# Attention stage: one normalisation and a fifth factor head move from VectorE to GpSimd, and some steps change their head

## Chip, cores and metric

One core of a Trainium2 chip runs the whole kernel. The metric is the device time of one execution in microseconds; lower is better. Engines are called by their names in the profile: PE is TensorE (PEld its weight loads), DVE VectorE, ACT ScalarE, POOL GpSimd, SP the queue that issues DMAs.

## What is computed

Four residual stages over x of 8 x 1024 rows of 256; the change touches only the first, attention with a learned relation bias:

```python
q, k, v = (x @ W.T + b).reshape(b, s, h, hd)          # 16 heads of 16
attn_scores = einsum('bihd,bjhd->bhij', q, k) / scale
logits = li[:, :, None, :] + lj[:, None, :, :] + rel_b # 3 relations per pair (i, j)
relation_probs = softmax(logits)
bias = einsum('bijk,hk->bhij', relation_probs, logical_bias)
gate = sigmoid(x @ gate_W.T + gate_b)
attn_weights = softmax(attn_scores + gate * bias)
out = einsum('bhij,bjhd->bihd', attn_weights, v) @ Wo.T + bo
x = x + out                                            # attention's x is layernorm(x)
```

An fp8-like linear layer, a Mamba mixer and a tail of MLPs follow; they are the same before and after.

## The kernel before, in words

Attention works in 64 tiles t of 128 query rows against the 1024 keys of their batch. Every engine runs its own hand-written list of steps per tile, `body`, in which `u` counts the 16 heads; semaphores alone tie the lists together. Two tiles are one turn of a loop.

For head h the steps are: the factor pass f(h), which writes rho[h] * P1 + P0 into one of eight row buffers `srow`. VectorE does it in one instruction from PSUM (`dve_f`, L491). For the heads in POOL_HEADS, 1, 4, 8 and 12, GpSimd does it in two from SBUF (`pool_f`, L408 and L410), with a wait on its own first result between them and a wait for the row buffer's last transposes (t_ok). Then s(h), `dve_s` (L502): add the scores from PSUM `ps_s`, of which there is only one, and take the row's minimum. VectorE's order is f(u+1), s(u), extras of u, so between s(u) and s(u+1) lie the extras of u and f(u+2). PE's next scores (L647) wait for s(u). Then e(h) on ScalarE (L576), the exponential with that minimum; eight transposes on PE (L658), which come two heads behind; their copies by ScalarE (L585); and PE's product with V (L670).

Beside this each tile t prepares two other tiles. The relation factors of tile t+1: `dve_rel` at u = 0 and 1 (L474, L477) write RT; GpSimd `pool_rel` (L382, twice), ScalarE `act_rel` at u = 1, 3, 4; GpSimd `pool_sum` (L387, L391); ScalarE `act_y0` at u = 7 and 8, Ln and Exp (L568, L571), of which R2 is an approximate reciprocal; then a Newton pass: GpSimd `pool_t` (L395), VectorE `dve_y` at u = 10 (L482); then GpSimd's two products `pool_p` (L400), which raise p_ok. ScalarE's `act_p` (L537, u = 13) copies one of them into PSUM `ps_p`, for VectorE's f(0) of the next tile.

The projections of tile p = t+9: `dve_ln` at u = 2 (L432, L434, L436: mean, variance), GpSimd `pool_rstd` (L368), VectorE `dve_xn` at u = 5 (L440), PE's transposes and products through the one PSUM bank `ps_m`, ScalarE `act_d` (eT, L528), GpSimd `pool_gT` (L414: eT becomes min(eT, HUGE) + 1), VectorE `dve_qk` at u = 14 (L447, waits for gT_ok and for PE), and in the next tile ScalarE `act_hi` (L542), GpSimd `pool_rem` (L372), `act_mid`, `pool_lo` (L376). `dve_v` (L455, u = 4) adds V's bias, `pool_ge` (L418), `dve_gate` (u = 13) and `pool_kappa` (L422) make the gate. The output of tile t-1: `act_o` (L589, u = 5) copies ps_o, `dve_norm` (L508, L510) divides, `pool_xrb` (L427) adds the bias to the residual, `dve_out` adds the rest. The last eight tiles have no projections (`pro` is false).

GpSimd's order in a tile is: f(4), rem, rel, rel, rstd, lo, f(8), sum, sum, f(12), xrb, t, ge, p, p, eT, f(1) of the next tile, kappa.

Of the kernel before, what the change touches and what calls it, by code (L numbers as in the profile page):

```python
# [18 lines left out]
NT = S // P  # L19
# [30 lines left out]
def attention(nc, x_in, wqk, wvg, bqk, rows, ident_in, parts_d, x_out):  # L50
# [4 lines left out]

    AHEAD = NT + 1
    NROW = 8
    POOL_HEADS = (1, 4, 8, 12)
    DVE_HEADS = tuple(h for h in range(H) if h not in POOL_HEADS)
    NPH, NDH = len(POOL_HEADS), len(DVE_HEADS)  # L60
    LAG = 2
# [2 lines left out]
    with ExitStack() as ctx:  # L64
# [301 lines left out]
        def pool_rstd(pool, p):  # L366
            alone(pool, ln_step, 3 * p + 3, pool_own)
            nc.gpsimd.tensor_tensor(rstd[:], ve[:], mhalf[:], ALU.pow).then_inc(rstd_ok, 1)  # L368

        def pool_rem(pool, p):  # L370
            alone(pool, hi_ok, p + 1, pool_own)
            nc.gpsimd.tensor_tensor(qkf[:], qkf[:], parts[:, 0], ALU.subtract).then_inc(rem_ok, 1)  # L372
# [57 lines left out]
        def dve_ln(dve, p, k):  # L430
            wait(dve, x_in_s, 16 * p + 16)
            nc.vector.bn_stats(stats[:], xt[:, k, :]).then_inc(ln_step, 1)  # L432
            alone(dve, ln_step, 3 * p + 1, dve_own)
            nc.vector.bn_aggr(mv[:], stats[:]).then_inc(ln_step, 1)  # L434
            dve.wait_ge(ln_step, 3 * p + 2)
            nc.vector.tensor_scalar(ve[:], mv[:, 1:2], LN_EPS, None, ALU.add).then_inc(ln_step, 1)  # L436

        def dve_xn(dve, p, k):
            wait(dve, rstd_ok, p + 1)
            nc.vector.tensor_scalar(xn[:], xt[:, k, :], mv[:, 0:1], rstd[:, 0:1],  # L440
                                    ALU.subtract, ALU.mult).then_inc(x_free, 1)

        def dve_qk(dve, p):
            wait(dve, gT_ok, p + 1)
# [404 lines left out]
        @block.gpsimd  # L849
        def _(pool):  # L850
            def start(pool):
                pool_g_rstd(pool, 0)
                pool_rstd(pool, NT)
                pool_g_rstd(pool, 1)
                pool_gT(pool, NT)
                pool_rem(pool, NT)
                pool_lo(pool, NT)
                pool_f(pool, 0, 0, 1)

            def body(pool, t, k, par, ib, pro, post, look, before):  # L860
                pool_f(pool, t, k, 4)
                if followed(t, pro):
                    pool_rem(pool, t - 1 + AHEAD)
                for n in range(2 * look):
                    pool_rel(pool, t + 1, 1 - k, after(par, ib, 1), n)
                if pro:
                    pool_rstd(pool, t + AHEAD)
                if followed(t, pro):
                    pool_lo(pool, t - 1 + AHEAD)
                pool_f(pool, t, k, 8)  # L870
                for n in range(2 * look):
                    pool_sum(pool, t + 1, 1 - k, n)
                pool_f(pool, t, k, 12)
                if post:
                    pool_xrb(pool, t - 1)
                if look:
                    pool_t(pool, t + 1)
                if pro:
                    pool_ge(pool, t + NT)
                for n in range(2 * look):  # L880
                    pool_p(pool, t + 1, 1 - k, n)
                if pro:
                    pool_gT(pool, t + AHEAD)
                if look:
                    pool_f(pool, t + 1, 1 - k, 1)
                if pro:
                    pool_kappa(pool, t + NT, 1 - par, ib)

            def finish(pool):
                pool_xrb(pool, TILES - 1)  # L890

            nc.gpsimd.memset(mhalf[:], -0.5)
            for v in V:
                nc.gpsimd.memset(v[:, :, :, HD + 1:2 * HD], 0.0)
                nc.gpsimd.memset(v[:, :, :, HD:HD + 1], 1.0).then_inc(v_ok, 1)
            pool.wait_ge(v_ok, 2)
            run(pool, start, body, finish)

        @block.vector
        def _(dve):  # L900
# [51 lines left out]
            def body(dve, t, k, par, ib, pro, post, look, before):  # L952
                for u in range(H):
                    if u + 1 < H:
                        dve_f(dve, t, k, u + 1)
                    dve_s(dve, t, k, after(par, ib, 0), u)
                    if look and u < 2:
                        dve_rel(dve, t + 1, 1 - k, after(par, ib, 1), u)
                    if pro and u == 2:
                        dve_ln(dve, t + AHEAD, 1 - k)  # L960
                    if u == 3 and (not isinstance(t, int) or t >= 2):
                        dve_out(dve, t - 2)
                    if pro and u == 5:
                        dve_xn(dve, t + AHEAD, 1 - k)
                    if pro and u == 4:
                        dve_v(dve, t + NT, 1 - par, ib)
                    if post and u == 6:
                        dve_norm(dve, t - 1)
                    if look and u == 10:
                        dve_y(dve, t + 1)  # L970
                    if pro and u == 13:
                        dve_gate(dve, t + NT)
                    if pro and u == 14:
                        dve_qk(dve, t + AHEAD)
                    if look and u == 15:
                        dve_f(dve, t + 1, 1 - k, 0)
# [48 lines left out]
            for i, (c, sgn, inv) in enumerate(((cdiff[:, 0, :], csgn, cn), (cdT[:], sgT, cdT))):  # L1025
# [10 lines left out]
                                    w_qk[:, :, 0:D].rearrange("p c (h d) -> p c h d", d=HD),  # L1036
                                    cinv[:].unsqueeze(1).unsqueeze(3).broadcast_to([P, DC, H, HD]), ALU.mult
                                    ).then_inc(w_ready, 1)
            dve_xn(dve, NT, 0)
            dve_g_ln(dve, 1)  # L1040
            dve_g_xn(dve, 1)
            dve.wait_ge(w_ready, 2)
# [2 lines left out]
        @block.scalar  # L1045
        def _(act):
            def start(act):
                act.wait_ge(w_ready, 1)
                act_g_t(act, 0)
                act_xT(act, NT)  # L1050
                act_g_d(act, 0)
                act_g_e(act, 0)
                act_d(act, NT, NT)
                for s in range(2):
                    act_g_hi(act, 0, s)
                act_g_t(act, 1)
                for s in range(2):
                    act_g_mid(act, 0, s)
                act_g_ge(act, 0)
                act_g_d(act, 1)  # L1060
                act_g_e(act, 1)
                act_rel(act, 0, 0, 0, 0)
                act_rel(act, 0, 0, 0, 1)
                act_rel(act, 0, 0, 0, 2)
                for s in range(2):
                    act_g_hi(act, 1, s)
                for s in range(2):
                    act_g_mid(act, 1, s)
                for step in range(2):
                    act_y0(act, 0, step)  # L1070
                act_p(act, 0, 0)
                act_hi(act, NT)
                act_g_ge(act, 1)
                act_mid(act, NT)
                act.wait_ge(g_st, 16 * 8)

            def body(act, t, k, par, ib, pro, post, look, before):
                for u in range(H):
                    act_e(act, t, u)
                    if post and u == 5:  # L1080
                        act_o(act, t - 1)
                    if pro and u == 7:
                        act_xT(act, t + AHEAD)
                    if look and u in (7, 8):
                        act_y0(act, t + 1, u - 7)
                    if u >= LAG:
                        act_at(act, t, u - LAG)
                    elif post:
                        act_at(act, t - 1, H + u - LAG)
                    if u == 0 and (not isinstance(t, int) or t >= 2):  # L1090
                        act_aT(act, t - 2)
                    if followed(t, pro) and u == 0:
                        act_hi(act, t - 1 + AHEAD)
                    if followed(t, pro) and u == 2:
                        act_mid(act, t - 1 + AHEAD)
                    if look and u in (1, 3, 4):
                        act_rel(act, t + 1, 1 - k, after(par, ib, 1), (1, 3, 4).index(u))
                    if pro and u == 6:
                        act_gate(act, t + NT, 1 - par, ib)
                    if pro and u == 10:  # L1100
                        act_d(act, t + AHEAD, after(par, ib, AHEAD))
                    if look and u == 13:
                        act_p(act, t + 1, 1 - k)

            def finish(act):
                for u in range(H - LAG, H):
                    act_at(act, TILES - 1, u)
                act_aT(act, TILES - 2)
                act_o(act, TILES - 1)
                act_aT(act, TILES - 1)  # L1110

            act.preload_act_table_set("natural_log_exp_and_others")
            act.sem_inc(at_ok, 2)
            run(act, start, body, finish)
# [1298 lines left out]
```

## Time and profile before

| | us |
|---|---|
| median of 3 runs (lowest, highest) | 6042.34 (6040.91, 6044.29) |
| the profiled execution | 6042.3 |
| its span, first to last instruction | 6040.5 |
| busy in the span: PE, DVE, ACT, POOL | 5365.8, 4701.5, 4409.7, 3704.9 |

Attention takes about the first 2850 us of the span. The granted clock of PE is 1.00 through its middle. A timeline row gives start, duration, engine, line, operation, output <- inputs with partitions x elements, a count, and in brackets the idle time just before it and what ended it. Successive instructions of one engine overlap a little, so steps are best read from start to start.

### The profile page before, as it was taken

The numbers are of one execution on the slowest core, as the hardware profiler recorded it, in microseconds if no ns is written. First come the engines' busy times: TensorE is split into PE (matmuls) and PEld (weight loads), VectorE is DVE, ScalarE is ACT, GpSimd is POOL, SyncE is SP. The second block draws the span as 40 slices with busy tenths as digits, with TensorE's granted clock in tenths as the row PEclk, the third lists the DMA queues.
The fourth block names the chain that finished last, engine by engine and source line by source line (L and its number), as shares of the span: only waits on it lengthen the run. The fifth ranks groups of instructions, "written<-read, shape, count | busy, mean of one in ns | idle before, by whom it ended". The sixth has DMA issues, their size and how long they took to land. (4 is left out here: it accounts for less than half of the span.)

```text
span 6040.5 us, 114022 instructions
## 1 busy us (share of the span) xinstructions
PE 5365.8 (89%) x40162; PEld 3532.6 (58%) x40162; DVE 4701.5 (78%) x6099; ACT 4409.7 (73%) x7005; POOL 3704.9 (61%) x2010
## 2 busy tenths in 40 slices
PE   6888888898989898888799869999999979999999
PEld 4666666666666666655344345555555546666665
DVE  6999999999999999998888679999999942122221
ACT  4999999999999999999366678888888821111111
POOL 3888888888888888875100079999999930000000
PEclk8999999999999999999899889999999989999999
DMA  2121121212112121200355555555555521111110
GB/s 74 28 49 31 28 51 28 51 28 51 28 34 45 30 48 31 46 17 14 129 190 211 187 211 187 208 208 191 195 201 207 184 101 42 45 35 35 35 35 11
DMA packets 461255, 537.80 MB, mean 89 GB/s; under 512 B 237537, under 2 KB 337761, under 8 KB 460785
## 3 DMA queue, kind: packets, MB, share of 16 engines
q1 hardware_dynamic: 460784, 531.75, 28.0%
q8 instruction: 268, 4.39, 0.3%
q14 instruction: 203, 1.66, 0.1%
HBM read 370.31 MB, written 161.35 MB: 88 GB/s over the span
## 5 line engine op out<-in xcount | busy, mean ns | idle before, releaser
L502 DVE CUSTOM_DVE_ANT_0 srow<-srow,ps_s,small 128x1024 f32<-128x1024 f32 x1024 | 1304.0, 1273 | 63.5 <-issue 34.6
L576 ACT ACTIVATE srow<-srow,nmax 128x1024 f32<-128x1024 f32 x1024 | 1200.0, 1172 | 87.3 <-DVE nmax L502 78.3
L585 ACT COPY AT<-ps_t 128x512 f32<-128x512 f32 x2048 | 1110.5, 604 | 19.8 <-PE ps_t L658 18.8
L658 PEld LDWEIGHTS ps_t<-ident,srow 128*128 128x128 f32 x8192 | 954.9, 141 | 224.2 <-issue 36.3
L658 PE MATMUL ps_t<-ident,srow 128*128 128x128 f32 x8192 | 1068.7, 273 | 2.8 <-ACT AT L585 2.4
L1977 POOL TENSOR_TENSOR c_hc<-c_hs,c_cs 128x1024 f32<-128x1024 f32 x432 | 1009.9, 2364 | 61.2 <-DVE c_hs L2079 59.1
L491 DVE SCALAR_TENSOR_TENSOR srow<-ps_p,rho,R 128x1024 f32<-128x1024 f32 x768 | 975.3, 1270 | 0.0
L1938 PE MATMUL c_ps_y<-c_hc,c_ident 128*128 128x512 f32 x2048 | 944.8, 594 | 29.9 <-DVE c_y L2062 21.4
L2079 DVE TENSOR_TENSOR_SCAN c_hs<-c_da,c_pd 128x1024 f32<-128x1024 f32 x384 | 860.1, 2273 | 54.6 <-PE c_pd L1929 54.6
L647 PE MATMUL ps_s<-K,Q 96*128 96x512 bf16 x2048 | 617.1, 383 | 291.2 <-DVE nmax L502 265.3
L2022 ACT ACTIVATE c_sT<-c_dxT,c_bT 128x256 f32<-128x256 f32 x1536 | 668.4, 494 | 107.0 <-PE c_pd L1929 96.9
L410 POOL TENSOR_TENSOR srow<-srow,R 128x1024 f32<-128x1024 f32 x256 | 608.1, 2375 | 46.9 <-POOL srow L408 46.9
L670 PE MATMUL ps_o<-AT,V 128*32 128x128 f32 x16384 | 607.4, 278 | 0.0
L2215 POOL TENSOR_TENSOR d_rstd<-d_ve,d_mhalf 128x4 f32<-128x4 f32 x16 | 16.3, 1017 | 899.1 <-DVE d_ve L1222 899.1
L1938 PEld LDWEIGHTS c_ps_y<-c_hc,c_ident 128*128 128x128 f32 x2048 | 359.5, 190 | 344.9 <-issue 314.0
L1929 PEld LDWEIGHTS c_pd<-c_ident,c_sT 128*128 128x128 f32 x3072 | 353.9, 142 | 340.0 <-issue 198.1
L1929 PE MATMUL c_pd<-c_ident,c_sT 128*128 128x128 f32 x3072 | 407.4, 276 | 106.8 <-DVE c_hc L2086 79.6
L670 PEld LDWEIGHTS ps_o<-AT,V 128*32 128x32 f32 x16384 | 401.3, 109 | 129.3 <-issue 128.5
L2013 ACT ACTIVATE c_da<-c_dt,c_a_neg 128x1024 f32<-128x1024 f32 x384 | 435.8, 1135 | 1.7 <-issue 1.7
L647 PEld LDWEIGHTS ps_s<-K,Q 96*128 96x128 bf16 x2048 | 144.4, 97 | 476.0 <-DVE nmax L502 342.9
L1970 POOL TENSOR_TENSOR c_db<-c_dx,c_bs 128x1024 f32<-128x1024 f32 x128 | 302.1, 2361 | 121.4 <-DMA c_bs<-bc_d 121.4
L2242 DVE TENSOR_TENSOR d_x<-d_ps_y,d_y 128x512 f32<-128x512 f32 x32 | 22.1, 691 | 438.6 <-PE d_ps_y L2317 438.6
(256 smaller groups left out, 8576.5 us busy)
## 6 DMA issues: line engine op xcount, KB each, us to landing
c_cs<-bc_d SPq DMA_DIRECT2D x256, 512.0 KB, 4.3
c_bs<-bc_d SPq DMA_DIRECT2D x64, 512.0 KB, 6.5
Q<-parts_d SPq DMA_DIRECT2D x384, 64.0 KB, 2.3
parts_d<-parts SPq DMA_DIRECT2D x57, 384.0 KB, 3.4
K<-parts_d SPq DMA_DIRECT2D x168, 128.0 KB, 4.4
sz_d<-b_sz SPq DMA_DIRECT2D x16, 1024.0 KB, 7.1
xv_d<-b_xv SPq DMA_DIRECT2D x16, 1024.0 KB, 7.8
dt_d<-b_ab SPq DMA_DIRECT2D x16, 1024.0 KB, 4.2
```

The source lines that it names most:

```text
L491: nc.vector.scalar_tensor_tensor(r[:], ps_p[:], rho[:, h:h + 1], R[k][0][:], ALU.mult, ALU.add).then_inc(fd_ok, 1)
L502: nc.vector.tensor_tensor_reduce(r[:], r[:], ps_s[:], small[:, slot, h:h + 1], BIG, ALU.add, ALU.min, nmax[:, h % NROW:h % NROW + 1]).then ...
L576: nc.scalar.activation(r[:], r[:], ACT.Exp, scale=-1.0, bias=nmax[:, h % NROW:h % NROW + 1]).then_inc(e_ok, 1)
L585: nc.scalar.copy(AT[h % NAT][:, HG * half:HG * half + HG, :], ps_t[:, half]).then_inc(at_ok, 1)
L647: last = nc.tensor.matmul(ps_s[:, n * 512:(n + 1) * 512], Q6[k][:, h, :], K6[:, h, n * 512:(n + 1) * 512], start=True, stop=True)
L658: last = nc.tensor.transpose(ps_t[:, half, i, :], rows_sb[h % NROW][:, j * P:(j + 1) * P], ident[:])
L670: last = nc.tensor.matmul(ps_o[32 * i:32 * i + 32, j, :], V[par][:, n, h, :], AT[h % NAT][:, n, :], start=(n == 0), stop=(n == NT - 1))
L1929: last = nc.tensor.transpose(pd[:, c, k * P:(k + 1) * P], src[:, k, c * P:(c + 1) * P], ident[:])
L1938: last = nc.tensor.matmul(ps_y[:, c, cut], ident[:], hc[place((n, c)) % NHC][:, cut], start=n == 0, stop=n == NS - 1)
L1977: nc.gpsimd.tensor_tensor(hc[place((n, c)) % NHC][:], hs[place((n, c)) % NHS][:], cs[n % NCS][:], ALU.mult).then_inc(hp_ok, 1)
L2022: last = nc.scalar.activation(sT[i % NSC][:, k, :], dxT[p][:, k, :], ACT.Copy, scale=bT[p][:, k, n:n + 1])
L2079: nc.vector.tensor_tensor_scan(h, gain, push, 0.0, ALU.mult, ALU.add).then_inc(h_ok, 1)
```

## The change

GpSimd takes the factor passes of heads 1, 4, 7, 10 and 13 instead of 1, 4, 8 and 12; VectorE does f(8) and f(12) and no longer f(7), f(10) and f(13). The normalised x (`xn`) is written by GpSimd (`pool_xn`), right after rstd and after a wait on its own result. `dve_ln` waits for the xn before (x_free) ahead of overwriting mean and variance. On VectorE V's bias goes from u = 4 to 5, the Newton pass `dve_y` from u = 10 to 11; on ScalarE the copy of ps_o goes from u = 5, just after e(5), to the end of u = 4. GpSimd's order becomes: f(4), rem, rel, rel, rstd, xn, lo, f(7), sum, sum, f(10), t, f(13), ge, xrb, p, p, eT, f(1), kappa.

```diff
-    POOL_HEADS = (1, 4, 8, 12)
+    POOL_HEADS = (1, 4, 7, 10, 13)
+        def pool_xn(pool, p, k):
+            alone(pool, rstd_ok, p + 1, pool_own)
+            nc.gpsimd.tensor_scalar(xn[:], xt[:, k, :], mv[:, 0:1], rstd[:, 0:1],
+                                    ALU.subtract, ALU.mult).then_inc(x_free, 1)
...
         def dve_ln(dve, p, k):
             wait(dve, x_in_s, 16 * p + 16)
             nc.vector.bn_stats(stats[:], xt[:, k, :]).then_inc(ln_step, 1)
+            alone(dve, x_free, p + 2, dve_own)
             alone(dve, ln_step, 3 * p + 1, dve_own)
...
-        def dve_xn(dve, p, k):
-            wait(dve, rstd_ok, p + 1)
-            nc.vector.tensor_scalar(xn[:], xt[:, k, :], mv[:, 0:1], rstd[:, 0:1],
-                                    ALU.subtract, ALU.mult).then_inc(x_free, 1)
...
                 if pro:
                     pool_rstd(pool, t + AHEAD)
+                    pool_xn(pool, t + AHEAD, 1 - k)
                 if followed(t, pro):
                     pool_lo(pool, t - 1 + AHEAD)
-                pool_f(pool, t, k, 8)
+                pool_f(pool, t, k, 7)
                 for n in range(2 * look):
                     pool_sum(pool, t + 1, 1 - k, n)
-                pool_f(pool, t, k, 12)
+                pool_f(pool, t, k, 10)
+                if look:
+                    pool_t(pool, t + 1)
+                pool_f(pool, t, k, 13)
+                if pro:
+                    pool_ge(pool, t + NT)
                 if post:
                     pool_xrb(pool, t - 1)
-                if look:
-                    pool_t(pool, t + 1)
-                if pro:
-                    pool_ge(pool, t + NT)
...
                     if pro and u == 5:
-                        dve_xn(dve, t + AHEAD, 1 - k)
-                    if pro and u == 4:
                         dve_v(dve, t + NT, 1 - par, ib)
                     if post and u == 6:
                         dve_norm(dve, t - 1)
-                    if look and u == 10:
+                    if look and u == 11:
                         dve_y(dve, t + 1)
...
-                    if post and u == 5:
-                        act_o(act, t - 1)
...
+                    if post and u == 4:
+                        act_o(act, t - 1)
```

The prologue's one `dve_xn` becomes a `pool_xn` in GpSimd's `start` in the same way.

## Rows read from the trace of the kernel before

**Rows 1.** Busy us (x instructions) of each engine, 1500 to 2000 us; then clock, DMA
```profile
1500.00:2000.00 500.00, 447.29 (x5386) 337.28 (x5385) 474.41 (x691) 485.64 (x742) 422.50 (x256) 1.00 0.16 35
```

**Rows 2.** Timeline of ScalarE, one tile: start us, us, engine line, [idle before]
```profile
1191.10 1.15 ACT L576 ACTIVATE srow<-srow,nmax 128x1024 f32<-128x1024 f32 x1 [0.46 <-DVE nmax L502]
...
1205.88 1.07 ACT L568 ACTIVATE R<-RT 128x1024 f32<-128x1024 f32 x1
...
1208.84 1.08 ACT L571 ACTIVATE R<-R 128x1024 f32<-128x1024 f32 x1
...
1234.38 1.15 ACT L576 ACTIVATE srow<-srow,nmax 128x1024 f32<-128x1024 f32 x1 [0.46 <-DVE nmax L502]
```

**Rows 3.** Timeline of GpSimd over the same tile
```profile
1202.35 2.38 POOL L391 TENSOR_TENSOR RT<-RT,R 128x1024 f32<-128x1024 f32 x1 [0.27 <-POOL RT L387]
1204.70 1.12 POOL L408 TENSOR_SCALAR srow<-R,rho 128x1024 f32<-128x1024 f32 x1
...
1208.34 0.74 POOL L427 TENSOR_TENSOR xr<-xr,row 128x256 f32<-128x256 f32 x1
1210.09 2.38 POOL L395 TENSOR_TENSOR RT<-RT,R 128x1024 f32<-128x1024 f32 x1 [1.01 <-ACT R L571]
1212.44 0.28 POOL L418 TENSOR_SCALAR ge<-ge 128x16 f32<-128x16 f32 x1
1213.91 4.72 POOL L400 TENSOR_TENSOR R<-R,R 128x1024 f32<-128x1024 f32 x2 [1.19 <-DVE R L482]
1218.61 1.06 POOL L414 TENSOR_SCALAR eT<-eT 128x256 f32<-128x256 f32 x1
...
1223.29 0.23 POOL L422 TENSOR_TENSOR small<-cn,gate 128x16 f32<-128x16 f32 x1
...
1230.74 2.23 POOL L372 TENSOR_TENSOR qkf<-qkf,parts 128x512 f32<-128x512 f32 x1 [2.93 <-ACT parts L542]
```

**Rows 4.** Timeline of VectorE, end of this tile and start of the next
```profile
1222.73 0.61 DVE L447 SCALAR_TENSOR_TENSOR qkf<-ps_m,b_qk,eT 128x128 f32<-128x128 f32 x2 [0.37 <-PE ps_m L613]
...
1223.59 1.27 DVE L502 CUSTOM_DVE_ANT_0 srow<-srow,ps_s,small 128x1024 f32<-128x1024 f32 x1
...
1227.48 0.88 DVE L474 TENSOR_SCALAR RT<-Dj,small 128x1024 f32<-128x1024 f32 x1
...
1230.68 1.27 DVE L477 SCALAR_TENSOR_TENSOR RT<-Dj,small,RT 128x1024 f32<-128x1024 f32 x1
...
1233.07 1.26 DVE L502 CUSTOM_DVE_ANT_0 srow<-srow,ps_s,small 128x1024 f32<-128x1024 f32 x1
```

**Rows 5.** Timeline of VectorE: the Newton pass, V's bias and xn
```profile
1212.51 1.23 DVE L482 SCALAR_TENSOR_TENSOR R<-RT,R 128x1024 f32<-128x1024 f32 x1 [0.18 <-POOL RT L395]
...
1239.65 0.42 DVE L455 TENSOR_TENSOR V<-ps_m,row 128x256 f32<-128x256 f32 x1 [0.41 <-PE ps_m L635]
...
1242.47 0.64 DVE L440 TENSOR_SCALAR xn<-xt,mv,rstd 128x256 f32<-128x256 f32 x1
```

**Rows 6.** VectorE against GpSimd: timeline rows, and L372's ns min/median/max
```profile
93.42 2.35 POOL L410 TENSOR_TENSOR srow<-srow,R 128x1024 f32<-128x1024 f32 x1 [0.18 <-POOL srow L408]
...
94.56 2.29 DVE L477 SCALAR_TENSOR_TENSOR RT<-Dj,small,RT 128x1024 f32<-128x1024 f32 x1
...
L372 POOL TENSOR_TENSOR qkf<-qkf,parts x57: 1152/2233/2252, 84.9 to 2529.1; 128x512 f32<-128x512 f32 x57
...
2734.96 2.36 POOL L410 TENSOR_TENSOR srow<-srow,R 128x1024 f32<-128x1024 f32 x1 [0.18 <-POOL srow L408]
...
2736.66 1.22 DVE L474 TENSOR_SCALAR RT<-Dj,small 128x1024 f32<-128x1024 f32 x1
```

**Rows 7.** Timeline of GpSimd in two of the last tiles, which project nothing
```profile
2719.91 2.36 POOL L395 TENSOR_TENSOR RT<-RT,R 128x1024 f32<-128x1024 f32 x1 [1.51 <-ACT R L571]
...
2762.00 2.37 POOL L395 TENSOR_TENSOR RT<-RT,R 128x1024 f32<-128x1024 f32 x1 [1.52 <-ACT R L571]
```

More of the change, by code:

```diff
@@ L853, in start @@
                 pool_rstd(pool, NT)
+                pool_xn(pool, NT, 0)
                 pool_g_rstd(pool, 1)
@@ L1038, in _ @@
                                     ).then_inc(w_ready, 1)
-            dve_xn(dve, NT, 0)
             dve_g_ln(dve, 1)
```

## The prediction

> **What bounds the kernel now.** Only the attention stage is touched, so I first read the busy time of the engines over 500 us in its middle [rows 1]: ScalarE 485.6 of 500, VectorE 474.4, TensorE 447.3, GpSimd 422.5. No engine is free, and ScalarE alone would need 0.971 of the time. The order of events decides, so I read the timeline of one tile, engine by engine. Call s(h) the VectorE reduction of head h (L502), f(h) the factor pass in front of it (L491 on VectorE, L408 with L410 on GpSimd), e(h) ScalarE's exponential (L576). The same e(2) of two tiles starts at 1191.10 and 1234.38 [rows 2]: a period of 43.28 us, and 64 tiles make the stage. The loop that closes this period runs as follows. e(2) waits 0.46 us for VectorE; from there ScalarE never stops until Ln (L568) at 1205.88 and Exp (L571) at 1208.84 [rows 2]. GpSimd's product pool_t waits for that Exp and starts at 1210.09 [rows 3]. Then GpSimd sits idle 1.19 us for VectorE's Newton pass (L482), does the two products of L400 and eT (L414), and reaches f(1) of the next tile [rows 3]. VectorE's qkf (L447) starts at 1222.73, s(15) follows at 1223.59, and s(2) of the next tile at 1233.07 [rows 4], which frees e(2) at 1234.38. GpSimd has one large slack, 2.93 us before L372, where it has run ahead of ScalarE [rows 3].
>
> **The change, part by part, in one tile.** *VectorE loses* one factor pass of the twelve and xn, 0.64 us [rows 5], and dve_v one head later no longer meets its 0.41 us wait for TensorE [rows 5]. A factor pass costs about 1.2 us: from L502 at 1223.59 to L474 at 1227.48 [rows 4] there are three such passes, s(15), f(0) and s(0), with a wait of 0.2 among them, in 3.89. That is 2.2 us less, from 41.1 us busy. But nothing of it counts if VectorE then waits at L447.
>
> *GpSimd gains* a factor pass, 3.64 us (1204.70 to 1208.34 [rows 3]), and xn. The trace shows no subtract-and-multiply on GpSimd with two column scalars. Nearest rows: mult-and-add of 1024 columns 1.12, and of 16 columns (min, add) 0.28; interpolated, 256 columns are 0.28 + 0.84/4 = 0.5. Against it min-and-add of just 256 columns takes 1.06 [rows 3]. Bounds 0.28 and 1.06; I take 0.5, since arithmetic without a min is nearer to L408, plus 0.18 for the wait on its own previous result, as L410 shows in front of it [rows 6]. Is it on the path? The sums (L391) end at 1202.35 + 2.38 = 1204.73, and Ln starts at 1205.88, held by ScalarE's own work: 1.15 of cover. 0.18 + 0.5 + 0.05 for a semaphore fits. Above 0.9 us xn would come through; at 1.06 it costs 0.17 per tile. The Trainium skill (GPSIMD Engine Reference, § 4.1 Engine selection) calls one-input work on GpSimd roughly line rate; L408 agrees, L414 with a quarter of the columns in the same 1.1 us does not. By the rule the sum below stands at 6112; by L414 it would be 6122.
>
> *The new order on GpSimd.* Between Exp and eT stood pool_t, ge, an idle wait for the Newton pass, two products, eT. Now it is pool_t, f(13), ge, xrb, two products, eT. The idle wait goes (the Newton pass finds f(13) as cover), but 3.64 + 0.74 comes in. Chain from e(2):
> - to Ln 14.78, to the start of pool_t 4.21 (1210.09 - 1205.88) [rows 2, 3]: unchanged, ScalarE's own pace
> - pool_t 2.35, f(13) 3.64, ge 0.28, xrb 0.74, products 4.70 (1213.91 to 1218.61), eT 1.06 [rows 3]: 12.77
>
> So eT is ready 31.76 after e(2). Today L447 starts 1222.73 - 1191.10 = 31.63 after it, held by TensorE, with eT ready three us earlier. So even with all of VectorE's saving L447 starts at 31.76 + 0.06. From there to the next e(2) it is 11.65, as before (1234.38 - 1222.73): rel steps, f(2), f(3) are the same. The period would be 43.47, less a few hundredths by which neighbours overlap: 43.4. GpSimd's chain has taken VectorE's place, and the 2.2 us are spent waiting for gT_ok.
>
> *The new collision.* The Newton pass L482 reads RT and R2, both in SBUF. L477 has the same form. Where L477 was issued at 94.56, while GpSimd's L410 ran until 95.77, it took 2.29 instead of 1.27: it ran only in the 1.08 after L410's end. Where it starts first, GpSimd waits: L372 takes 1.15 at the shortest and 2.23 in the median [rows 6], and it starts at 1230.74 [rows 3], just behind L477's start at 1230.68 [rows 4]; so a hold of about 1.07. Today L482 runs in GpSimd's idle time and costs nobody anything [rows 3, 5]. In the new order f(13) follows pool_t at once, 1212.44 to 1216.1 on this tile's clock. VectorE comes to L482 about two passes after the 1212.3 of today, so between 1214.1 and 1214.8: in the middle of f(13)'s L410. It waits for L410's end, then GpSimd's ge waits about 1.07 for L482; had it got in front of L410, GpSimd would lose the same. Nothing in GpSimd's chain absorbs it, as the chain is the bound. VectorE itself loses 1.4 to 2.0 there, which it has from the 2.2.
> The Trainium skill (GPSIMD Engine Reference, § 8 Key points) says the same in general: GpSimd shares its SBUF interfaces with VectorE instructions of two SBUF inputs; the rows of L477 and L372 bear it out, with 1.07 us.
>
> *Moves at no cost.* act_o one head earlier, norm with f(8) behind it, and the added wait on x_free in dve_ln (set most of a tile before; behind it s(3), which ScalarE doesn't lack): they lie before Ln, where ScalarE works without a gap. If the x_free wait did bind, s(3) and e(3) would be late by all of it. The prologue's xn moves once, under 1 us. GpSimd's slack before L372 shrinks from 2.93: from eT's end it does f(1), kappa, f(4), 3.62 + 0.22 + 3.64 = 7.5, while ScalarE's hi is ready 8.1 after it (1230.74 - 1222.73 + 0.06), so 0.6 is left.
>
> **Sum.** 43.4 + 1.07, less 0.05 for the handover = 44.4, +1.15 per tile. Last eight tiles have no projections and a period of 42.09 [rows 7]; there p_ok and the Newton pass meet the same collision, and I take the same 1 us. 61 tiles (64 less start and end) x 1.15 = 70. The profiled execution spans 6040.5 and took 6042.3, the median of the runs is 6042.34, so 6042 + 70 = 6112 us.
>
> **Rivals.**
> 1. *No collision*: L482 falls in the 0.18 gap before L410, or the hold isn't paid by GpSimd. For it: L482 never took over 1.23 today. Against: GpSimd was idle each time. Period 43.4, +0.12 x 61 = +7: 6050.
> 2. *Faster*: eT isn't late (GpSimd's chain shorter than its rows say), and ScalarE becomes the bound: 43.28 x 0.971 = 42.04, plus the 0.46 before e(2) that stays, 42.5; -0.78 x 61 = -48: 5995. For it: VectorE's relief of 2.2 us is real. Against: the chain is made of durations that hardly vary.
> 3. *Much slower*: L474 (rel step 0) is itself held by a running L410: 1.22 where one ended 0.66 into it [rows 6]. It will be issued 4.8 after eT's end (1227.48 - 1222.73 + 0.06); f(4)'s L408 runs 3.84 to 4.96, its L410 from 5.14 for 2.4. L474 slips into the gap. If VectorE is later by 0.35, it waits out L410: +2.4 on s(1), s(2), e(2), and the whole chain. 61 x 3.6 = +219: 6260.
>
> xn at 1.06 adds 0.17 x 61 = 10: 6122, within the first case; so do 0.1 us either way per tile in the tie between VectorE and GpSimd at L447 (6 us), and the last tiles.
>
> **Chances.** Forecast (6085 to 6150) 0.69; rival 1 0.11; rival 2 0.10; rival 3 0.10. The range 6045 to 6150 takes in rival 1 and leaves 0.2 out. Within 0.2% (12 us, about what a measurement can tell here) is rival 1: same 0.11, faster 0.10, slower 0.79.
>
> **What would show it.** Period of L502's tiles 44.4; VectorE idle before L447 <- GpSimd eT L414 (today TensorE L613); L482 with a mean of 2.5 us or more, or L410/L418 lengthened by 1 us; GpSimd busy over 95%, its wait before L372 under 1 us; ScalarE's share falling to about 94.5%, with new idle time before act_p or e(12) to e(15); xn on GpSimd near 0.5. Wrong if L447 still waits for TensorE, or if L482 stays 1.23 and its neighbours on GpSimd too.

## The result and the profile after

The changed kernel takes 6127.35 us (median of 4 runs, 6125.14 to 6129.7) against 6042.21: a ratio of 1.014, with a 95% interval of 1.0128 to 1.0153. It is 85 us slower; 70 were forecast. Its profiled execution spans 6124.3 us against 6040.5. Line numbers of the new file are higher, from L372 (the new xn) on: L483 is the Newton pass, L448 qkf, L503 the head reduction, L413 and L415 GpSimd's factor pass, L400 pool_t, L405 the products, L423 ge, L432 xrb, L419 eT, L377 rem, L475 and L478 the rel steps.

The busy times over the same 500 us as [rows 1] (us, PE, PEld, DVE, ACT, POOL, clock, DMA) show the shift of work: GpSimd 95% busy instead of 84.5%, VectorE and ScalarE both less busy. No engine has more to do than the span allows, yet each tile is longer.

```profile
1500.00:2000.00 500.00, 441.38 (x5226) 326.05 (x5226) 457.80 (x650) 476.55 (x722) 475.32 (x282) 1.00 0.19 38
```

GpSimd's timeline answers [rows 3]. The stretch from pool_t to eT has f(13) in it, and ge, 0.28 before, takes 1.26:

```profile
1189.32 1.13 POOL L413 TENSOR_SCALAR srow<-R,rho 128x1024 f32<-128x1024 f32 x1
1190.63 2.36 POOL L415 TENSOR_TENSOR srow<-srow,R 128x1024 f32<-128x1024 f32 x1 [0.18 <-POOL srow L413]
1192.96 1.26 POOL L423 TENSOR_SCALAR ge<-ge 128x16 f32<-128x16 f32 x1
1194.19 0.72 POOL L432 TENSOR_TENSOR xr<-xr,row 128x256 f32<-128x256 f32 x1
1194.88 4.72 POOL L405 TENSOR_TENSOR R<-R,R 128x1024 f32<-128x1024 f32 x2
1199.58 1.06 POOL L419 TENSOR_SCALAR eT<-eT 128x256 f32<-128x256 f32 x1
...
1208.69 2.10 POOL L377 TENSOR_TENSOR qkf<-qkf,parts 128x512 f32<-128x512 f32 x1 [0.28 <-ACT parts L543]
...
1216.20 1.23 POOL L372 TENSOR_SCALAR xn<-xt,mv,rstd 128x256 f32<-128x256 f32 x1 [0.22 <-POOL rstd L368]
```

VectorE's timeline of the same stretch answers [rows 4, 5]:

```profile
1191.18 2.90 DVE L483 SCALAR_TENSOR_TENSOR R<-RT,R 128x1024 f32<-128x1024 f32 x1
1194.00 1.27 DVE L503 CUSTOM_DVE_ANT_0 srow<-srow,ps_s,small 128x1024 f32<-128x1024 f32 x1
...
1200.67 0.61 DVE L448 SCALAR_TENSOR_TENSOR qkf<-ps_m,b_qk,eT 128x128 f32<-128x128 f32 x2 [0.53 <-POOL eT L419]
...
1205.43 0.75 DVE L475 TENSOR_SCALAR RT<-Dj,small 128x1024 f32<-128x1024 f32 x1
...
1235.65 2.89 DVE L483 SCALAR_TENSOR_TENSOR R<-RT,R 128x1024 f32<-128x1024 f32 x1
```

The Newton pass asks at 1191.18. L415 runs until 1190.63 + 2.36 = 1192.99; the pass ends 1191.18 + 2.90 = 1194.08, 1.09 later; ge, next on GpSimd, has its start recorded at 1192.96 and ends at 1194.22. The wait is no idle time in the trace, it is inside the durations. Then qkf waits 0.53 for eT, where it waited for TensorE before. The distance of the two L483 rows is the period, 44.47 us against 43.28. In the view of waits qkf (L447 before, L448 now) no longer waits for TensorE but for GpSimd's eT, 0.53 a tile, and of all 64 Newton passes the median is that of these rows (ns min/median/max, first and last start):

```profile
L483 DVE SCALAR_TENSOR_TENSOR R<-RT,R x64: 1224/2896/3233, 77.8 to 2884.5; 128x1024 f32<-128x1024 f32 x64
```

ScalarE's row of Ln shows the price of xn: it now waits for the sums (L396); the cover of 1.15 us is used up.

```profile
1227.24 1.06 ACT L569 ACTIVATE R<-RT 128x1024 f32<-128x1024 f32 x1 [0.19 <-POOL RT L396]
```

By tile, from one rel step to the next, the first three distances add nothing (128.1 against 128.2 us), the 53 regular ones 61.2, the last seven 16.8, where a period of 42.1 became 44.7. The rest of the 84 us lies behind: the last L502 is at 2854.8 before and the last L503 at 2934.5, 80 us later, and some 4 us more lie in later stages whose code is the same. Why these stages take longer is not shown. It goes with the fifth head: from the last head reduction to the end of the span it is 3189.8 to 3194.2 us in the profiled executions of all kernels with five heads on GpSimd, and 3183.3 to 3186.0 in those with four.

### The profile page after: what moved, and what is told of

Its sections match the earlier page's. It is cut to its first block and busy times, and to the rows that moved or that the text cites. A ratio compares the mean times of both kernels' runs of the same rounds, so it can differ in the third digit from the quotient of the medians.

```text
span 6124.3 us, 114392 instructions
## 1 busy us (share of the span) xinstructions
PE 5409.7 (88%) x40162; PEld 3528.9 (58%) x40162; DVE 4686.4 (77%) x5978; ACT 4431.5 (72%) x7005; POOL 4063.6 (66%) x2195
## 3 DMA queue, kind: packets, MB, share of 16 engines
q14 instruction: 230, 1.88, 0.1%
## 5 line engine op out<-in xcount | busy, mean ns | idle before, releaser
L503 DVE CUSTOM_DVE_ANT_0 srow<-srow,ps_s,small 128x1024 f32<-128x1024 f32 x1024 | 1304.0, 1273 | 186.6 <-issue 159.3
L492 DVE SCALAR_TENSOR_TENSOR srow<-ps_p,rho,R 128x1024 f32<-128x1024 f32 x704 | 893.7, 1269 | 0.0
L415 POOL TENSOR_TENSOR srow<-srow,R 128x1024 f32<-128x1024 f32 x320 | 775.5, 2423 | 59.9 <-POOL srow L413 59.9
L671 PE MATMUL ps_o<-AT,V 128*32 128x128 f32 x16384 | 611.6, 279 | 0.0
L671 PEld LDWEIGHTS ps_o<-AT,V 128*32 128x32 f32 x16384 | 404.3, 110 | 130.5 <-issue 129.5
L413 POOL TENSOR_SCALAR srow<-R,rho 128x1024 f32<-128x1024 f32 x320 | 361.4, 1129 | 13.3 <-PE ps_t L659 10.9
```

Source lines behind the costliest of these rows:

```text
L415: nc.gpsimd.tensor_tensor(r[:], r[:], R[k][0][:], ALU.add).then_inc(fp_ok, 1)
L492: nc.vector.scalar_tensor_tensor(r[:], ps_p[:], rho[:, h:h + 1], R[k][0][:], ALU.mult, ALU.add).then_inc(fd_ok, 1)
L503: nc.vector.tensor_tensor_reduce(r[:], r[:], ps_s[:], small[:, slot, h:h + 1], BIG, ALU.add, ALU.min, nmax[:, h % NROW:h % NROW + 1]).then ...
L671: last = nc.tensor.matmul(ps_o[32 * i:32 * i + 32, j, :], V[par][:, n, h, :], AT[h % NAT][:, n, :], start=(n == 0), stop=(n == NT - 1))
```

## Experiments

Two theories were set against each other. **A, the chain**: the period is the loop e(2), Ln, Exp, pool_t, f(13) with the Newton pass's hold, ge, xrb, the products, eT, qkf, s(15), s(2), e(2). **B, the full engine**: GpSimd at 95% is simply full and its total sets the period. The kernel before was timed beside each run, at 6041 to 6043 us; ratios are to it. A period below is the usual distance of two first rel steps in the regular tiles.

**One half of the change without the other.** The changed kernel with dve_xn in the place of pool_xn, and without the wait on x_free:

```diff
                     if pro and u == 5:
+                        dve_xn(dve, t + AHEAD, 1 - k)
                         dve_v(dve, t + NT, 1 - par, ib)
...
-                    pool_xn(pool, t + AHEAD, 1 - k)
```

> The changed kernel with xn back on VectorE (at u = 5, ahead of V's bias, in the gap that f(7) left); heads and order on GpSimd stay changed. Theory A, the chain: the period (44.47 us in the changed kernel) is set by e(2), Ln, pool_t, f(13) with the Newton pass's hold, ge, xrb, the products, eT, L448 (qkf), s(2). xn and its wait (1.23 + 0.22) touch it only by the 0.20 that Ln now waits for the sums: period about 44.27, time 6127 - 0.2 x 56 = 6116, and GpSimd's wait before its rem step grows from 0.27 to about 1.5. Theory B, the full engine: GpSimd has hardly any idle time left, so its total sets the period, and all of the 1.42 comes back: 43.05, 6047.

Measured 6113.97 us, ratio 1.0114 (1.0098 to 1.0131), period 44.19. A gave 6116 and 44.27, B 6047. GpSimd got 1.45 us per tile back and the kernel 0.28: a full engine is not the bound. One detail missed: the wait before rem did not grow to 1.5. The freed time stands before pool_t, where GpSimd waits for Exp. The tile of these rows is one of the few irregular ones, and its wait of 2.46 is too large; the median of the regular tiles is 1.69, against 0.55 in the changed kernel:

```profile
1218.72 2.39 POOL L391 TENSOR_TENSOR RT<-RT,R 128x1024 f32<-128x1024 f32 x1 [0.27 <-POOL RT L387]
...
1227.23 2.38 POOL L395 TENSOR_TENSOR RT<-RT,R 128x1024 f32<-128x1024 f32 x1 [2.46 <-ACT R L571]
...
1233.24 1.25 POOL L418 TENSOR_SCALAR ge<-ge 128x16 f32<-128x16 f32 x1
```

That is consistent with the chain, since the time from eT to the next hi does not contain xn; my expectation had placed it wrongly. It also didn't foresee that xn on VectorE would meet f(7)'s second instruction: it takes 1.56 in the median there, 0.41 at the shortest. VectorE had the time to spare, as its wait for eT in front of qkf stayed at 0.53.

The other half, on the kernel before (pool_xn itself and the wait on x_free in dve_ln are as in the change):

```diff
                 if pro:
                     pool_rstd(pool, t + AHEAD)
+                    pool_xn(pool, t + AHEAD, 1 - k)
...
-                    if pro and u == 5:
-                        dve_xn(dve, t + AHEAD, 1 - k)
```

> The kernel before with one part of the change alone: xn on GpSimd behind rstd, with the wait on x_free in dve_ln. Heads 1, 4, 8, 12 and all orders stay. Theory A: xn and its wait, 1.45, lie ahead of the sums, which had 1.15 of cover before Ln, so Ln and what follows is 0.3 to 0.35 later: period 43.27 to about 43.6, time 6042 + 18 = 6060. Rival: VectorE's relief of 0.56 counts, and the period falls towards 42.9, 6022.

Measured 6056.37, ratio 1.0021 (1.0012 to 1.0031), period 43.64. xn costs 0.37 us per tile there, and VectorE's relief brings nothing: it only waits longer for pool_t in front of the Newton pass, 0.94 instead of 0.49 (medians). The fifth head with its order and the small moves costs 71 us (6114 - 6043), xn alone 14; together 85, as measured.

**The collision by itself.**

```diff
-            nc.vector.scalar_tensor_tensor(R2[:], RT[:], 2.0, R2[:], ALU.subtract, ALU.mult).then_inc(rel_y, 1)
+            nc.vector.scalar_tensor_tensor(R2[:], ps_p[:], 2.0, R2[:], ALU.subtract, ALU.mult).then_inc(rel_y, 1)
```

> The changed kernel, but the Newton pass reads PSUM's ps_p in the place of RT in SBUF: same form, length and waits, only one SBUF input. Its values are meaningless, so the relation factors are wrong; no other work differs. Theory A: the pass takes 1.27 instead of 2.90, ge 0.28 instead of 1.25, the period falls by about 1.0 to 43.5, time 6127 - 61 = 6066. If the meeting of the two engines is harmless and only the longer order counts (theory C), the period stays 44.4 to 44.5 and the time within 6 us of 6127.

This kernel leaves out the true Newton update and serves for its time alone. Measured 6051.61, ratio 1.0012 (1.0003 to 1.0022), period 43.53, and 41.2 in the last six tiles. With one operand in PSUM the pass takes 1.22, ge behind it 0.29, qkf comes 0.94 us earlier in its tile and still waits for eT (VectorE, then GpSimd):

```profile
1210.52 1.22 DVE L483 SCALAR_TENSOR_TENSOR R<-ps_p,R 128x1024 f32<-128x1024 f32 x1
...
1219.05 0.61 DVE L448 SCALAR_TENSOR_TENSOR qkf<-ps_m,b_qk,eT 128x128 f32<-128x128 f32 x2 [1.02 <-POOL eT L419]
```
```profile
1209.96 2.38 POOL L415 TENSOR_TENSOR srow<-srow,R 128x1024 f32<-128x1024 f32 x1 [0.18 <-POOL srow L413]
1212.31 0.29 POOL L423 TENSOR_SCALAR ge<-ge 128x16 f32<-128x16 f32 x1
```

So the collision is worth 6127 - 6052 = 75 of the 85 us: 0.94 in each of some 54 tiles, and 3.5 on average in each of the last six, far more than the 1 that was forecast. What stays in a regular tile, 43.53 against 43.28, is the chain itself with xn in it. In the last tiles, which have neither eT nor qkf, the relief of VectorE does count once the collision is gone: 41.2 against 42.1 before.

**The chain's contents moved, not removed.**

```diff
-                if post:
-                    pool_xrb(pool, t - 1)
                 for n in range(2 * look):
                     pool_p(pool, t + 1, 1 - k, n)
...
                     pool_f(pool, t + 1, 1 - k, 1)
+                if post:
+                    pool_xrb(pool, t - 1)
```

> The changed kernel with xrb (0.72 us on GpSimd) moved out of the stretch between pool_t and eT to behind f(1) of the next tile; nothing is removed. Theory A: eT is ready 0.7 earlier, VectorE's qkf had waited 0.53 for it, so the period falls by about 0.5 to 43.95, time near 6097. Theory B (GpSimd's total sets the period): its work is the same, no change, 6127.

Measured 6176.87, ratio 1.0219 (1.0202 to 1.0236): neither 6097 nor 6127, but 50 us slower than the changed kernel; the period is 45.06, and 46.2 in about every third tile, which stays unexplained. The half microsecond was won as expected, qkf no longer waits for eT. The start of the next tile shows what was lost (GpSimd, then VectorE):

```profile
1224.76 1.12 POOL L413 TENSOR_SCALAR srow<-R,rho 128x1024 f32<-128x1024 f32 x1
1226.07 2.60 POOL L415 TENSOR_TENSOR srow<-srow,R 128x1024 f32<-128x1024 f32 x1 [0.18 <-POOL srow L413]
1228.62 1.16 POOL L377 TENSOR_TENSOR qkf<-qkf,parts 128x512 f32<-128x512 f32 x1
```
```profile
1225.23 1.21 DVE L475 TENSOR_SCALAR RT<-Dj,small 128x1024 f32<-128x1024 f32 x1
...
1228.74 2.12 DVE L478 SCALAR_TENSOR_TENSOR RT<-Dj,small,RT 128x1024 f32<-128x1024 f32 x1
```

xrb behind f(1) made f(4) late. The first rel step waits out L413 (1.21 in the place of 0.75), f(4) runs up to rem, which now starts 0.12 ahead of the second rel step and holds it for 0.85. Both lie between s(0) and s(2), on the loop: from qkf to e(2) it is now 12.82, where it was 11.52. The slack that GpSimd had before rem, 0.28, is less than the 0.73 of xrb; I read it as what had kept the two engines apart.

The other way round, into the idle 0.55 ahead of pool_t:

> The changed kernel with xrb (0.72) moved the other way, to ahead of pool_t, where GpSimd sits idle 0.55 for Exp; so it ends what stands between pool_t and eT, and f(4) of the next tile is not pushed later as it was when xrb stood behind f(1). Chain theory: pool_t 0.17 later, eT 0.55 earlier; the Newton pass waits out f(13)'s second instruction 0.17 later, and VectorE, 6.15 us from s(12) to qkf, becomes the last at qkf: period 44.47 - 0.35 = 44.1, time about 6106. If GpSimd's total work set the period, nothing changes: 44.47, 6127. A third way out: VectorE is then 0.2 later against GpSimd, and the first rel step meets f(4)'s second instruction: period over 45.

```diff
+                if post:
+                    pool_xrb(pool, t - 1)
                 if look:
                     pool_t(pool, t + 1)
                 pool_f(pool, t, k, 13)
...
-                if post:
-                    pool_xrb(pool, t - 1)
```

Measured 6107.48, ratio 1.0109 (1.0091 to 1.0127), period 44.16: the chain's 6106 and 44.1, with no wait for eT left in front of qkf. The work is the same as in the changed kernel, only the place differs; B gave no change and falls.

**The fifth head elsewhere, the pass under a one-input instruction.**

```diff
-    POOL_HEADS = (1, 4, 7, 10, 13)
+    POOL_HEADS = (1, 4, 7, 10, 12)
...
-                pool_f(pool, t, k, 13)
+                pool_f(pool, t, k, 12)
...
-                    if look and u == 11:
+                    if look and u == 10:
                         dve_y(dve, t + 1)
```

> The changed kernel with GpSimd's fifth head 12 in the place of 13, and the Newton pass back at u = 10. VectorE then asks for the pass while GpSimd runs the first, one-input instruction of f(12), which did not meet two-input VectorE work in any row so far (ge ran beside the pass in the kernel before, both at full speed). Theory A with that: the pass takes about 1.27 and is over when f(12)'s second instruction starts, no hold; period as without the collision, 43.5, time near 6052. If one-input work of GpSimd holds the pass too, the pass takes over 2 us and the period is 44.0 to 44.5.

Measured 6130.94, ratio 1.0147 (1.0129 to 1.0165), period 44.57: my hope of 6052 was wrong. Both instructions were free to go when pool_t ended. The pass took its 1.22, and it was GpSimd's one-input L413 that waited, 2.19 in the place of 1.12; f(12) came late and s(12) waited for it:

```profile
1191.90 1.22 DVE L483 SCALAR_TENSOR_TENSOR R<-RT,R 128x1024 f32<-128x1024 f32 x1 [0.84 <-POOL RT L400]
...
1196.82 1.28 DVE L503 CUSTOM_DVE_ANT_0 srow<-srow,ps_s,small 128x1024 f32<-128x1024 f32 x1 [1.29 <-POOL srow L415]
```
```profile
1191.86 2.19 POOL L413 TENSOR_SCALAR srow<-R,rho 128x1024 f32<-128x1024 f32 x1
1194.23 2.37 POOL L415 TENSOR_TENSOR srow<-srow,R 128x1024 f32<-128x1024 f32 x1 [0.18 <-POOL srow L413]
```

In the kernel before, ge beside the pass was no counterexample: it had only 16 columns, started first, and was over 0.21 after the pass's recorded start.

**Is the same loop the bound of both kernels?** ScalarE's Exp goes one step up, ahead of e(8):

```diff
-                    if look and u in (7, 8):
-                        act_y0(act, t + 1, u - 7)
+                    if look and u == 7:
+                        act_y0(act, t + 1, 0)
                     if u >= LAG:
                         act_at(act, t, u - LAG)
                     elif post:
                         act_at(act, t - 1, H + u - LAG)
+                    if look and u == 7:
+                        act_y0(act, t + 1, 1)
```

> The kernel before with one step moved: ScalarE's Exp of the reciprocal (L571) directly behind the transposes' copy that follows Ln, ahead of e(8) in the place of behind it, 1.05 us earlier. If the loop e(2), Ln, Exp, pool_t, Newton pass, s(11) to s(15), s(2) sets the period of the kernel before as well, pool_t comes up to 1.0 earlier, VectorE loses its 0.47 wait at the Newton pass: period 43.27 - 0.45 = 42.8, time near 6016. If ScalarE's own work were the bound, no change: 6042.

> The changed kernel with the same move of ScalarE's Exp, 1.05 us earlier. Chain theory: pool_t follows f(10) at once, 0.55 to 0.6 earlier, and everything up to qkf with it: period 43.9, time near 6093. If GpSimd's total work set the period: gain none, 6127.

On the kernel before: 6009.05, ratio 0.9945 (0.9928 to 0.9963), period 42.74 (42.8 and 6016 expected). On the changed kernel: 6084.2, ratio 1.0071 (1.0053 to 1.0089), period 43.87 (43.9 and 6093 expected). No work was taken away in either. The first is the fastest kernel of this study, 32 us below the kernel before timed beside it. In it GpSimd goes into pool_t without a wait and then waits for the pass, which is where VectorE now is late: its own wait in front of the pass, 0.49 in the median before, is gone, and that is why 1.05 earlier brings only 0.53. The wait of 1.96 in these rows is that of a slightly irregular tile; the median is 1.64, against 1.19:

```profile
1198.51 2.39 POOL L395 TENSOR_TENSOR RT<-RT,R 128x1024 f32<-128x1024 f32 x1
1200.87 0.28 POOL L418 TENSOR_SCALAR ge<-ge 128x16 f32<-128x16 f32 x1
1203.11 4.71 POOL L400 TENSOR_TENSOR R<-R,R 128x1024 f32<-128x1024 f32 x2 [1.96 <-DVE R L482]
```

**Can the fifth head pay at all?** This is the changed kernel with the PSUM operand, xrb ahead of pool_t and the early Exp, the three diffs above.

> The changed kernel with three things at once: the Newton pass reads PSUM's ps_p in the place of RT (its values are meaningless), xrb stands ahead of pool_t, and ScalarE's Exp comes 1.05 us earlier. Chain theory: pool_t at 26.1 as now, the hold (1.0) and xrb (0.7) gone from behind it: eT ends at 38.1, VectorE's own path reaches qkf at 37.6, period 42.9, time near 6016: the fifth head on GpSimd doesn't pay even then against the kernel before with the early Exp (42.74, 6009). If the fifth head's relief of VectorE counts once the collision is gone, the period falls under 42.5, 5995.

Measured 6051.54 as the median of ten executions, ratio 1.0046 (1.0021 to 1.0072). They spread far more than those of any other kernel here: six took 6048 to 6052, three 6087 to 6094, one 6110. In the profiled one, of 6048, most tiles have the expected 42.91, but in five tiles at the start and again in nine from 2076 us on the period is about 44.6. The first rel step (VectorE) tells the two apart, by where it falls against f(4) (GpSimd):

```profile
1988.23 0.75 DVE L475 TENSOR_SCALAR RT<-Dj,small 128x1024 f32<-128x1024 f32 x1
1988.58 2.65 POOL L415 TENSOR_TENSOR srow<-srow,R 128x1024 f32<-128x1024 f32 x1 [0.18 <-POOL srow L413]
...
2120.34 2.37 POOL L415 TENSOR_TENSOR srow<-srow,R 128x1024 f32<-128x1024 f32 x1 [0.18 <-POOL srow L413]
2120.50 2.77 DVE L475 TENSOR_SCALAR RT<-Dj,small 128x1024 f32<-128x1024 f32 x1
2165.09 2.77 DVE L475 TENSOR_SCALAR RT<-Dj,small 128x1024 f32<-128x1024 f32 x1
```

At 1988.23 it comes 0.35 ahead of f(4)'s second instruction, at 2120.50 it comes 0.16 behind it, waits it out, and that repeats itself from tile to tile. What starts and ends such a stretch is not shown. That is rival 3 of the prediction, in another kernel. Longer stretches of it could make the executions of 6087 to 6110: at 1.7 us a tile, 6110 would take some 36 more such tiles (an estimate). They were not profiled, so this is not shown. Even without it 42.91 is above the 42.74 of the kernel before with the early Exp; that no other order lets the fifth head pay isn't shown.

**The small moves alone**, on the kernel before:

> The kernel before with only the change's small moves that leave GpSimd alone: V's bias on VectorE at u = 5 (behind xn) and ScalarE's copy of ps_o at the end of u = 4. The prediction put them at no cost, since ScalarE works without a gap from e(2) to Ln: period 43.27, time within 6 us of 6041. If VectorE's path through heads 4 to 7 counted, its 0.4 us wait for TensorE would be saved and the period fall to about 42.9, 6018.

```diff
                     if pro and u == 5:
                         dve_xn(dve, t + AHEAD, 1 - k)
-                    if pro and u == 4:
                         dve_v(dve, t + NT, 1 - par, ib)
...
-                    if post and u == 5:
-                        act_o(act, t - 1)
...
+                    if post and u == 4:
+                        act_o(act, t - 1)
```

Measured 6092.26, ratio 1.0085 (1.0068 to 1.0102), where no change was expected. With V's bias gone from in front, xn came 0.9 us earlier and into the middle of GpSimd's L410 (ns min/median/max; it was 404/642/2604 before):

```profile
L440 DVE TENSOR_SCALAR xn<-xt,mv,rstd x57: 407/1549/1907, 19.0 to 2544.7; 128x256 f32<-128x256 f32 x57
```

s(6) behind it came 0.4 later. ScalarE, which had no idle time from e(2) to Ln, then had to wait, 0.23 for VectorE at e(6) and 0.85 for TensorE's transposes behind it, and the period was 43.7 in some tiles and 44.7 to 44.9 in others. To separate it, the copy alone:

> The kernel before with ScalarE's copy of ps_o at the end of u = 4 and nothing else: the last run moved V's bias too, and with it xn came 0.9 us earlier and into GpSimd's running f(8), 1.55 in the place of 0.64. With the copy alone xn stays where it was: no cost and no gain, period 43.27, time within 6 us of 6042. If the copy's new place itself costs (ScalarE or TensorE), 6060 or more.

```diff
-                    if post and u == 5:
-                        act_o(act, t - 1)
...
+                    if post and u == 4:
+                        act_o(act, t - 1)
```

Measured 6042.66, ratio 0.9999 (0.999 to 1.0009). The copy's move is free. So the 50 us come with V's bias out of its place in front of xn; that it is the hold of xn is read from the trace, and V's bias was never moved on its own without xn next to it; in the changed kernel xn isn't on VectorE, and there the step stands in a gap.

## Why the prediction was right, point by point

- *What bounds the kernel before*: the loop through Exp, pool_t and the Newton pass, as read. The early Exp shows it: 0.53 us per tile from a step that removes no work. Behind the pass it runs through VectorE's own s(11) to s(15), since eT is ready 3.1 us before qkf.
- *VectorE's relief of 2.2 us counts nothing*: right in the regular tiles. It waits 0.53 before qkf, about 1.3 before s(9), and 1.7 inside the Newton pass. xn off VectorE alone made the kernel slower. In the last tiles it would have counted, 0.9 us each.
- *The chain without the collision, 43.4*: 43.53 measured in the kernel with the PSUM operand.
- *The hold, 1.07*: somewhat less, 0.97 in ge (1.25 against 0.28), 0.94 in the period when it was taken away.
- *Period 44.4*: 44.47, with the signs named in advance: qkf waits for eT, the pass takes 2.9, GpSimd is 95% busy, its wait before rem is 0.28. Two signs are off: ScalarE's share is 95.3%, not 94.5, and xn was not near 0.5. That the period fits within 0.1 is in part luck, as errors of opposite sign cancel: xn, put at nothing, adds 0.28; the hold is 0.1 smaller; and from qkf to e(2), taken as unchanged, it is 0.13 less, since the first rel step takes 0.75 in the place of 0.88. Medians over 42 regular tiles:

| us | forecast | changed kernel | with the PSUM operand |
|---|---|---|---|
| e(2) to Ln | 14.78 | 15.06 | 15.07 |
| Ln to pool_t | 4.21 | 4.19 | 4.19 |
| pool_t to the end of eT | 12.77 + 1.07 | 13.67 | 12.72 |
| end of eT to qkf | 0.06 | 0.04 | 0.03 |
| qkf to the next e(2) | 11.65 | 11.52 | 11.52 |
| period | 44.4, after overlap | 44.48 | 43.53 |

- *xn at 0.5 us*: wrong, 1.23, above the bound of 1.06 that I had drawn from the min-and-add. The term was mis-sized because I interpolated by columns from a mult-and-add, and the row of the right length was eT's. The step said that above 0.9 it would come through; it did: 0.28 per tile in the changed kernel, 0.37 on the kernel before. By the step's own rule it would be 0.33 (1.23 - 0.9).
- *The last tiles, +1 each*: wrong, +2.6, and 16.8 us came from the last tiles instead of the 9 in the sum (8 x 1.15). The forecast charged them only with what GpSimd loses. But with neither eT nor qkf VectorE waits for nothing of GpSimd's at the end of the tile, the path runs through VectorE, and VectorE loses the whole of its own wait. Against the kernel with the PSUM operand (44.72 and 41.17) the pass takes 1.94 more, s(14) comes another 1.35 later against s(12), and the first rel step takes 0.2 more; that is all of the 3.5. s(14)'s wait of 1.28 is for TensorE: its scores for s(13) had waited 2.30 for s(12), its transposes and 1.88 of products with V (L671) follow, and its scores for s(14) end at 2804.22. The 0.84 before s(15) is in all three kernels. (TensorE's rows, then VectorE's.)

```profile
2799.59 0.60 PE L648 MATMUL ps_s<-K,Q 96*128 96x512 bf16 x2 [2.30 <-DVE nmax L503]
2800.03 1.85 PE L659 MATMUL ps_t<-ident,srow 128*128 128x128 f32 x8
2801.81 1.88 PE L671 MATMUL ps_o<-AT,V 128*32 128x128 f32 x32
2803.62 0.60 PE L648 MATMUL ps_s<-K,Q 96*128 96x512 bf16 x2
```
```profile
2795.17 3.16 DVE L483 SCALAR_TENSOR_TENSOR R<-RT,R 128x1024 f32<-128x1024 f32 x1
2798.26 1.27 DVE L503 CUSTOM_DVE_ANT_0 srow<-srow,ps_s,small 128x1024 f32<-128x1024 f32 x1
...
2804.40 1.28 DVE L503 CUSTOM_DVE_ANT_0 srow<-srow,ps_s,small 128x1024 f32<-128x1024 f32 x1 [1.28 <-issue]
2806.53 1.28 DVE L503 CUSTOM_DVE_ANT_0 srow<-srow,ps_s,small 128x1024 f32<-128x1024 f32 x1 [0.84 <-issue]
```

- The 15 us between 70 and 85 are then: 8 in the last tiles, 4 in later stages of unchanged code, the rest behind the last rel step (1.6) and between the profiled execution (84 more) and the medians (85). The 53 regular distances gave 61.2, which is 1.15 each, as in the sum.
- *Moves at no cost*: right for the copy, untested for V's bias alone.
- *Rival 1, no collision*: 6050 forecast for it; the kernel that has none takes 6052. That fit is also partly luck: its last tiles gain 0.9 each, and its later stages take 8.5 us more. *Rival 3, a rel step held by f(4)*: it did not occur in the regular tiles, 0.75 there, but it was near: the step comes 0.35 ahead of f(4)'s second instruction (1205.43 against 1205.78), the margin that the prediction had named. Three small gains at once brought the rival out; moving xrb by one place brought out two similar holds.

The Trainium skill's rule of the shared SBUF interfaces (GPSIMD Engine Reference, § 8 Key points) held, and with a two-input VectorE instruction even one-input GpSimd work was held (2.19 us). The rule of the Trainium skill that GpSimd does one-input work roughly at line rate (GPSIMD Engine Reference, § 4.1 Engine selection) did not hold for xn: 256 columns in 1.23 us, 1024 columns of mult-and-add in 1.12.

## What to carry to other kernels

Moving work to an engine with idle time pays only where the loop that sets the period gets shorter: follow one period from event to event, and put the moved step where it lies outside that loop. Before placing a VectorE instruction with two SBUF operands, look at what GpSimd runs at that moment; idle time on GpSimd beside it can be what makes it cheap. When GpSimd is nearly full, the relative phase of the two engines is part of the schedule: here a move of 0.7 us of work out of the loop cost 50 us by a new meeting. Where an engine isn't waited for, as GpSimd at the end of the last tiles, look at what the other one loses by the same collision.

## What the runs showed of the hardware

- In these runs VectorE and GpSimd excluded each other by whole instructions where VectorE had two SBUF inputs, or ran a tensor_scalar of 256 or 1024 columns from SBUF to SBUF: one of them waited until the other was done, and the wait lay in its duration (the pass 2.90 for 1.22; ge 1.25 for 0.28; L413 2.19 for 1.12; the first rel step 2.77 for 0.75; xn on VectorE 1.55 for 0.41). With one operand of the pass in PSUM neither side waited (1.22 and 0.29).
- GpSimd's subtract-and-multiply with two column scalars took 1.23 us for 256 columns, more than mult-and-add took for 1024 (1.12).
- One execution of one program held two periods, 42.91 and about 44.6, the second for nine tiles on end, with the first rel step ahead of or behind the start of f(4)'s second instruction.
